# Causal attention's setup: a chunk is projected and split in the norm's own loop, two chunks behind the variances

## What is computed

```python
x = x + _L1_attn_ref(_layernorm(x, axis=-1), Wq, Wk, Wv, Wo)

def _L1_attn_ref(x, Wq, Wk, Wv, Wo):
    q, k, v = (x @ Wq.T), (x @ Wk.T), (x @ Wv.T)     # each to 16 heads of 8
    scores = q @ k.T / sqrt(8), masked so that a query sees no later key
    return (softmax(scores) @ v) @ Wo.T
```

## Time and profile before

| | us |
|---|---|
| median of 3 executions (5180.65 to 5180.82) | 5180.65 |
| the profiled execution | 5180.6 |
| its span in the trace | 5178.8 |
| norm, projection and split of the causal attention (first mean product to first score, L247 to L1397) | 3445.97 to 3535.48 |

### The profile page before, as it was taken

One profiled execution on the slowest core, in us unless ns is written; L12 is line 12 of the kernel. 1 busy time (PEld: TensorE's weight loads), 2 busy tenths in 40 slices (PEclk: granted clock), 3 DMA queues, 4 the chain that ended last, 5 costly groups with the idle time before them and its releaser, 6 DMA issues.

```text
span 5178.8 us, 175419 instructions
## 1 busy us (share of the span) xinstructions
PE 4973.2 (96%) x76384; PEld 3261.6 (63%) x76384; DVE 3878.4 (75%) x5096; ACT 3439.4 (66%) x5293; POOL 2705.8 (52%) x1425
## 2 busy tenths in 40 slices
PE   8899999999999999999999999987999999989999
PEld 5577777777777777777777777762333333267677
DVE  5888888888888888888888888836777777443333
ACT  2588888888888888888888877743655566621111
POOL 1877777777777777777777777721111111110000
PEclk8899999999999999999999999977999999979999
DMA  2011111111111112111111111113111111010000
GB/s 75 25 41 47 33 33 44 43 35 34 36 51 35 30 35 56 31 35 34 44 43 35 30 48 34 35 28 74 20 20 20 20 20 20 1 37 4 4 4 4
DMA packets 98013, 168.30 MB, mean 32 GB/s; under 512 B 25081, under 2 KB 36866, under 8 KB 96898
## 3 DMA queue, kind: packets, MB, share of 16 engines
q1 hardware_dynamic: 94402, 148.06, 10.6%
q10 hardware_dynamic: 2880, 9.44, 1.2%
HBM read 47.44 MB, written 10.49 MB: 11 GB/s over the span
## 4 chain that ended last, share of the span: by engine, by line
PE 88%; ACT 3%; issue 2%; DVE 2%; POOL 1%; SPq 1%; DMA 1%; ACTq 0%; DVEq 0%; POOLq 0%
PE D L1333 7%; PE D L1264 7%; PE D L1189 6%; PE D L1275 6%; PE D L1417 5%; PE D L1439 5%; PE D L1292 5%; PE D L1125 5%; PE D L1243 5%; PE D L1520 5%; PE D L1397 4%; PE D L1301 4%; PE D L1170 4%; PE D L1303 4%; PE D L1178 3%; PE D L1205 2%
## 5 line engine op out<-in xcount | busy, mean ns | idle before, releaser
L475 POOL TENSOR_TENSOR rn<-ss,mhalf 128x33 f32<-128x33 f32 (+2 forms) x198 | 1095.8, 5534 | 329.3 <-DVE ss L861 314.8
L1000 DVE TENSOR_REDUCE mxp<-D 128x2 f32<-128x1024 f32 (+3 forms) x640 | 675.6, 1064 | 242.6 <-PE D L1397 130.9
L479 POOL TENSOR_TENSOR hh<-hh,rr 128x1024 f32<-128x1024 f32 x192 | 365.5, 1904 | 405.9 <-DVE rr L913 405.9
L747 ACT ACTIVATE V<-D 128x1024 f32<-128x1024 f32 (+3 forms) x426 | 381.8, 897 | 248.3 <-PE D L1417 242.7
L968 DVE TENSOR_TENSOR TOK<-D,wA 128x1024 f32<-128x1024 f32 x384 | 466.1, 1214 | 0.0
L859 DVE TENSOR_REDUCE ss<-TOK 128x32 f32<-128x2048 f32 x192 | 437.1, 2276 | 0.0
L1333 PE MATMUL D<-PTb,V 64*64 64x32 f32 x24576 | 406.5, 220 | 8.2 <-issue 7.3
L1333 PEld LDWEIGHTS D<-PTb,V 64*64 64x64 f32 x24576 | 381.6, 135 | 34.8 <-issue 10.8
L908 DVE TENSOR_REDUCE rs<-hh 128x16 f32<-128x1024 f32 x192 | 234.2, 1220 | 205.2 <-ACT hh L647 205.2
L675 ACT ACTIVATE V<-D 128x512 f32<-128x512 f32 x384 | 229.6, 598 | 218.9 <-PE D L1301 153.9
L483 POOL TENSOR_TENSOR XC<-XC,TOK 128x1024 f32<-128x1024 f32 x128 | 302.8, 2366 | 46.5 <-DVE TOK L968 46.5
(11 more groups left out here) (241 smaller groups left out, 11689.1 us busy)
## 6 DMA issues: line engine op xcount, KB each, us to landing
V<-V SPq DMA_DIRECT2D x936, 64.0 KB, 2.0
V<-V SPq DMA_DIRECT2D x192, 192.0 KB, 2.5
RB<-watt_dram SPq DMA_DIRECT2D x12, 512.0 KB, 4.2
X<-watt_dram SPq DMA_DIRECT2D x12, 512.0 KB, 3.8
parts_dram<-hh SPq DMA_DIRECT2D x48, 128.0 KB, 2.4
TOK<-parts_dram ACTq DMA_DIRECT2D x36, 128.0 KB
RA<-parts_dram SPq DMA_DIRECT2D x12, 384.0 KB
X<-parts_dram SPq DMA_DIRECT2D x12, 384.0 KB
```

The costliest lines, as they stand in the source:

```text
L475: pool.tensor_tensor(rn[:, st % 2, lo:hi], ss[:, st % 2, lo:hi], mhalf[:, lo:hi], ALU.pow).then_inc(s["powed"], 1)
L479: pool.tensor_tensor(sh, sh, rr[:, :].unsqueeze(2).to_broadcast([P, HEADS, 64]), ALU.mult).then_inc(s["pnorm"], 1)
L747: act.activation(PTE[i % 3][:, 2 * hp:2 * hp + 2, 0:CH - r * P], pair_of(("S", i + LAG, hp))[:, :].rearrange("p (h n) -> p h n", h=2)[:, : ...
L1000: dve.tensor_reduce(mxp[:, 2 * hp:2 * hp + 2, qt, kc], pair_of(("F", at, hp))[:, :].rearrange("p (h n) -> p h n", h=2)[:, :, 0:keys], AX.X ...
```

## The change

All engines but POOL and SP get the norm's second half (squares, variances, spreads, multiplications) and the projection and split as one loop over steps c. In step c, PE does variance c, spread c-1 and projection c-2; ACT does square c, then high parts and V copy of chunk c-2, then middle parts of chunk c-3; DVE does epsilon c, multiplication c-1, first subtractions of chunk c-2, then second subtractions of chunk c-3. The means and their subtractions stay a loop of their own ahead of it. Since banks 0 to 3 are in use by the norm, q and k go to banks 4 and 5 for every chunk, and v to bank 6 or 7; projection c therefore waits until the first subtractions of chunk c-1 (not c-2) are done. SPL and REST keep two slots. POOL's and SP's programs, and the number and shape of all instructions, are the same.

```diff
--- before.py
+++ after.py
@@ -717,19 +717,28 @@
                                       scr[1, p, hg * GH:(hg + 1) * GH, rep].rearrange("h d n -> d h n"))\
                            .then_inc(s[f"stacks_in{p}"], 16)
 
-            norm_scalar(act, K_ATT, lambda c: chunk(XC, c))
-            for c in range(NC):
-                act.wait_ge(s["c_proj"], c + 1)
-                if c >= 2:
-                    act.wait_ge(s[f"split_out{c % 2}"], 96 * (c // 2))
-                for qk in range(2):
-                    act.activation(SPL[:, c % 2, qk, 0, :], PB[(c % 2) * 3 + qk][:, :], ACT.Copy).then_inc(s["c_hi"], 1)
-                act.activation(VALL[:, c * NBLK:(c + 1) * NBLK, :].rearrange("p b f -> p (b f)"),
-                               PB[(c % 2) * 3 + 2][:, :], ACT.Copy).then_inc(s["c_vcopy"], 1)
-                for qk in range(2):
-                    act.wait_ge(s["c_rest"], 2 * c + qk + 1)
-                    act.activation(SPL[:, c % 2, qk, 1, :], REST[:, c % 2, qk, :], ACT.Copy).then_inc(s["c_mid"], 1)
-                if c == CB:
+            kn = K_ATT * NC
+            for c in range(NC + 3):
+                if c < NC:
+                    act.wait_ge(s["centered"], kn + c + 1)
+                    if c >= 2:
+                        act.wait_ge(s["var_ready"], kn + c - 1)
+                    act.activation(SQ[:, c % 2, :], chunk(XC, c), ACT.Square).then_inc(s["squared"], 1)
+                if 0 <= c - 2 < NC:
+                    u = c - 2
+                    act.wait_ge(s["c_proj"], u + 1)
+                    if u >= 2:
+                        act.wait_ge(s[f"split_out{u % 2}"], 96 * (u // 2))
+                    for qk in range(2):
+                        act.activation(SPL[:, u % 2, qk, 0, :], PB[4 + qk][:, :], ACT.Copy).then_inc(s["c_hi"], 1)
+                    act.activation(VALL[:, u * NBLK:(u + 1) * NBLK, :].rearrange("p b f -> p (b f)"),
+                                   PB[6 + u % 2][:, :], ACT.Copy).then_inc(s["c_vcopy"], 1)
+                if 0 <= c - 3:
+                    u = c - 3
+                    for qk in range(2):
+                        act.wait_ge(s["c_rest"], 2 * u + qk + 1)
+                        act.activation(SPL[:, u % 2, qk, 1, :], REST[:, u % 2, qk, :], ACT.Copy).then_inc(s["c_mid"], 1)
+                if c - 3 == CB:
                     for p in range(2):
                         act.wait_ge(s[f"split_out{p}"], 16 * 6 * CB // 2)
                     act.wait_ge(s["ones_ready"], 3)
@@ -973,19 +982,41 @@
             for st in range(-3, G + 7):
                 att_vector(st)
             dve.wait_ge(s["x2_ready"], NC)
-            norm_vector(dve, K_ATT, lambda c: chunk(XR, c), lambda c: chunk(XC, c))
-            for c in range(NC):
+            kn = K_ATT * NC
+
+            def split_rest(c):
+
                 if c >= 2:
                     dve.wait_ge(s[f"split_out{c % 2}"], 96 * (c // 2))
                 for qk in range(2):
 
                     dve.wait_ge(s["c_hi"], 2 * c + qk + 1)
-                    dve.tensor_tensor(REST[:, c % 2, qk, :], PB[(c % 2) * 3 + qk][:, :], SPL[:, c % 2, qk, 0, :],
+                    dve.tensor_tensor(REST[:, c % 2, qk, :], PB[4 + qk][:, :], SPL[:, c % 2, qk, 0, :],
                                       ALU.subtract).then_inc(s["c_rest"], 1)
+
+            def split_low(c):
+
                 for qk in range(2):
                     dve.wait_ge(s["c_mid"], 2 * c + qk + 1)
                     dve.tensor_tensor(SPL[:, c % 2, qk, 2, :], REST[:, c % 2, qk, :], SPL[:, c % 2, qk, 1, :],
                                       ALU.subtract).then_inc(s["c_low"], 1)
+
+            for c in range(NC):
+                dve.wait_ge(s["mean_ready"], kn + c + 1)
+                dve.tensor_tensor(chunk(XC, c), chunk(XR, c), PB[c % 2][:, :], ALU.subtract).then_inc(s["centered"], 1)
+            for c in range(NC + 3):
+                if c < NC:
+                    dve.wait_ge(s["var_ready"], kn + c + 1)
+                    if c >= 2:
+                        dve.wait_ge(s["rstd_ready"], kn + c - 1)
+                    dve.tensor_scalar(var_s[:, c % 2, :], PB[2 + c % 2][:, 0:NBLK], EPS, None, ALU.add).then_inc(s["var_copied"], 1)
+                if 1 <= c <= NC:
+                    dve.wait_ge(s["spread_ready"], kn + c)
+                    dve.tensor_tensor(chunk(XC, c - 1), chunk(XC, c - 1), PB[(c - 1) % 2][:, :], ALU.mult).then_inc(s["normed"], 1)
+                if 0 <= c - 2 < NC:
+                    split_rest(c - 2)
+                if 0 <= c - 3:
+                    split_low(c - 3)
             dve.wait_ge(s["c_vcopy"], NC)
             dve.memset(PB[4][:, :], 0.0).then_inc(s["o_zero"], 1)
 
@@ -1355,19 +1386,40 @@
                     values(st - 1)
             pe.wait_ge(s["layer_out"], G)
             pe.wait_ge(s["w1att_in"], 16)
-            norm_tensor(pe, K_ATT, lambda c: chunk(XR, c), "x2_ready", lambda c: c + 1)
-            for c in range(NC):
-                pe.wait_ge(s["normed"], K_ATT * NC + (c + 1 if c >= 2 else NC))
+            kn = K_ATT * NC
+
+            def project_c(c):
+
+                pe.wait_ge(s["normed"], kn + c + 1)
+                if c >= 1:
+                    pe.wait_ge(s["c_rest"], 2 * c)
                 if c >= 2:
-                    pe.wait_ge(s["c_rest"], 2 * (c - 1))
                     pe.wait_ge(s["c_vcopy"], c - 1)
-                bk = (c % 2) * 3
-                pe.matmul(PB[bk][:, :], wC[:, 0, :], chunk(XC, c), start=True, stop=True)
-                pe.matmul(PB[bk + 1][:, :], wC[:, 1, :], chunk(XC, c), start=True, stop=True)
+                pe.matmul(PB[4][:, :], wC[:, 0, :], chunk(XC, c), start=True, stop=True)
+                pe.matmul(PB[5][:, :], wC[:, 1, :], chunk(XC, c), start=True, stop=True)
                 for b in range(NBLK):
-                    m = pe.matmul(PB[bk + 2][:, b * P:(b + 1) * P], XC[:, c * CH + b * P:c * CH + (b + 1) * P], wC[:, 2, :],
+                    m = pe.matmul(PB[6 + c % 2][:, b * P:(b + 1) * P], XC[:, c * CH + b * P:c * CH + (b + 1) * P], wC[:, 2, :],
                                   start=True, stop=True)
                 m.then_inc(s["c_proj"], 1)
+
+            for c in range(NC):
+                pe.wait_ge(s["x2_ready"], c + 1)
+                if c >= 2:
+                    pe.wait_ge(s["centered"], kn + c - 1)
+                pe.matmul(PB[c % 2][:, :], mean_w, chunk(XR, c), start=True, stop=True).then_inc(s["mean_ready"], 1)
+            for c in range(NC + 2):
+                if c < NC:
+                    pe.wait_ge(s["squared"], kn + c + 1)
+                    if c >= 2:
+                        pe.wait_ge(s["var_copied"], kn + c - 1)
+                    for j in range(NBLK):
+                        m = pe.matmul(PB[2 + c % 2][:, j:j + 1], SQ[:, c % 2, j * P:(j + 1) * P], mean_w[:, 0:1],
+                                      start=True, stop=True)
+                    m.then_inc(s["var_ready"], 1)
+                if 1 <= c <= NC:
+                    spread(pe, K_ATT, c - 1)
+                if c >= 2:
+                    project_c(c - 2)
             pe.wait_ge(s["tri_ready"], 2)
             pe.wait_ge(s["o_zero"], 1)
             pe.wait_ge(s["c_rest"], 2 * NC)
```

## The result

The changed kernel takes 5197.25 us in the median of 8 executions (5187.81 to 5202.74), the kernel before 5180.65 (8 executions, 5172.38 to 5183.04): a ratio of 1.0033, 95% interval 1.0022 to 1.0043, so 11 to 22 us slower. The profiled execution took 5192.85 us, 12.25 more than the profiled one of before.

What follows compares the result with a forecast made beforehand. Bound: the split's copy, subtract, store ring with two slots. First split 14.76 us earlier, then 11.23 per chunk, an 18.01 store and a 9.09 round put first score 22.9 later: 5203.5 us, range 5187 to 5211.

Steps and rivals of the forecast that it cites:

- Serial order through PE and ScalarE: In the merged norm and split loop, each chunk's steps follow one another through both engines: 11.23 us per chunk.
- The lost slot: In the split's stores, a round of 9.09 us now serves one chunk, not two, and rules from chunk 6 on.
- The tail from there to the first score: From chunk 7's first copy: split 3.42, last subtraction 1.29, memset and semaphores 0.69; 5.40 us predicted.
- The clock: PE in the merged loop was taken at half clock, 0.50, giving 11.23 us per chunk; 8.32 with a full-clock projection.
- rival 2: PE mostly at full clock in the loop: +8.5 us, 5189.1; between, a clock rising inside a projection; chance 0.24.
- Store 4: Store of chunk 4's parts, beside group 0's key and query loads: taken as 18.01 us until chunk 6's first copy.
- the bound of 18.01 + 5: Upper bound in us for chunk 4's store meeting the loads; the lower bound was 5.67, no collision.
- POOL's ones: Memset of the first key stack, 6.92 us, gating the loads: a tie at half clock, some 2 us late at full.
- the time past the first score: Sign for the rest of the kernel: same length as before; a change of over 2 us would show the prediction wrong.
- Rival 4: The loads miss chunk 4's store, which lands in 5.67 us, PE at full clock: -3.8 us, 5176.8; chance 0.04.
- the lower half of rival 2: The part of rival 2 not above 5191, with PE mostly at full clock; 5189.1 us at full.
- slower: Whole kernel slower by more than the 0.2%, 10.4 us, that a measurement can tell from no change; chance 0.82.

Runs made afterwards that it cites:

- experiment 2: Kernel before with only the split staggered: first parts of chunk c, then middle and low parts of chunk c-1; stage 111.1 us, ratio 1.0040.
- experiment 8: Kernel before with only a third slot for the parts; stage 79.3 us, ratio 0.9981.
- experiment 6: Changed kernel with a third slot for the parts, its order kept; stage 101.1 us, ratio 1.0013.
- experiment 1: Changed kernel with chunk c-3's middle and low parts ahead of chunk c-2's first parts; stage 93.0 us, ratio 1.0016.
- experiment 3: Changed kernel with eight thrown-away bfloat16 products ahead of each variance from chunk 3 on; stage 98.2 us, ratio 1.0028.
- experiment 5: experiment 1 with POOL's ones of the first key stack filled ahead of the norm's powers; stage 90.3 us, ratio 0.9996.
- experiment 4: Changed kernel with group 0's query and key loads issued behind the last chunk instead of chunk 4; stage 117.5 us, ratio 1.0059.
- 7: experiment 5 with three slots and group 0's key loads issued ahead of chunk 5's copies; stage 81.7 us, ratio 0.9990.
- 9: Kernel before with four slots and group 0's query loads issued ahead of chunk 4's stores; stage 81.9 us, ratio 0.9976.
- experiment 10: Changed kernel, second parts first, ones early, four slots, key and query loads earlier, six thrown-away products per variance from chunk 3; stage 75.6 us, ratio 0.9969.

## Why the prediction was right, and where it was off

Direction, mechanism and range held: 5203.5 predicted (5187 to 5211), 5197.25 measured; for the stage +22.9 predicted and +15.1 measured. Part of the nearness is luck: two terms were off, one by 12.0 us too much and one by 4.4 too little.

- *Serial order through PE and ScalarE.* Shown: every copy of chunks 1 to 5 was released by the projection, every variance from chunk 4 on waited 3.22 us for its square (3.26 predicted), and turning the order round took 11.5 us away.
- *The lost slot.* Shown by experiment 2 (9.04 to 9.09 us per chunk against 9.09) and by chunk 7's copy, 9.04 after chunk 6's. The tail from there to the first score was 5.31 (5.40 predicted).
- *The clock, the term that was off.* I took 0.50 throughout. The first two projections ran at 1.00, so chunk 0's copy came 17.0 us into the stage (21.5 predicted) and chunk 1's 6.34 later (10.07); and each later projection caught the rise at its end, 10.27 us per chunk on average instead of 11.23. That is 4.5 + 3.7 + 3.8 = 12.0 us too much up to chunk 5. The third part is the case that rival 2 named, a clock that rises inside a projection.

The first two parts are not the change's doing. Up to projection 0 PE has the same instructions in both kernels, and the spread of chunk 0, ahead of any projection, took 1.11 us before and 0.65 after:

```profile
3458.57 1.11 PE L268 MATMUL D<-con,rstd 128*128 128x128 f32 x4 [0.54 <-POOL rstd L304]
```

```profile
3459.93 0.65 PE L268 MATMUL D<-con,rstd 128*128 128x128 f32 x4 [0.54 <-POOL rstd L304]
```

Experiment 8, in the order of before, had 0.65 there as well, and experiment 6, in the changed order, 1.11. So either order met either level at this point, and I had read only the one; in experiment 6 the first copy came at 20.3 us, near the predicted 21.5. Nor does the length of the wait alone decide how a burst begins. In experiment 1 every variance from chunk 3 on waited 2.18 us for its square:

```profile
3465.61 1.05 PE L1416 MATMUL D<-con,SQ 128*128 128x1 f32 x8 [2.18 <-ACT SQ L726]
...
3471.94 1.86 PE L1416 MATMUL D<-con,SQ 128*128 128x1 f32 x8 [2.18 <-ACT SQ L726]
...
3489.55 1.05 PE L1416 MATMUL D<-con,SQ 128*128 128x1 f32 x8 [2.18 <-ACT SQ L726]
```

The first and third of these ran at full clock, the second at half. The Trainium skill, "TensorE: Matmul & The Clock Gate", section "HAM oscillation", describes a loop of short bursts, each behind a wait for a DMA, in which every burst starts throttled. That held from the third burst of the changed kernel on (waits of 3.22 us, 0.57 to 0.58), not for the first two (waits of 2.2 us and less, 1.00). What sets the level in a given execution stays open.

- *Store 4.* 22.4 us instead of 18.01, 4.4 too little, inside the bound of 18.01 + 5. Together: -12.0 + 4.4 is -7.6, the sum's miss of 7.8 but for small change. In experiments 2 and 3 store 4 took 17.9 and 18.0 us beside the same loads; why 22.4 here, no run shows.
- *POOL's ones.* Counted as a tie at half clock and as 2 us late at full. They were 1.1 us late here, and filling them early took 2.7 us off the stage of experiment 1 (experiment 5).
- *A test that was none*: that the time past the first score should stay within 2 us. It changed by 4.5 us, which by that sign would have made the prediction wrong; but it scatters by 12 us among kernels that share that program.
- *A slip in the chances.* Rival 4 and the lower half of rival 2 are 0.04 + 0.12 = 0.16, not 0.14, and "slower" is then 0.80.
- *What I did not see:* that from the issue of the last loads 20 us and more go by. Had the split not been late, they would have set the end; I only had them as a hindrance to the stores.

## What to carry to other kernels

Staggering a producer's stages across chunks (first half of the next ahead of the second half of this one) uses up one buffer slot; where the slots are just enough to cover a store, it turns a round per two chunks into a round per chunk. Before overlapping two stages, ask what the second one really waits for at its end: once the slots sufficed, it was here the start of 2.4 MB of loads, and one more slot in the old order, a few lines, gave about as much (0.9981, interval 0.9972 to 0.9991) as the reordering with the same slots (0.9990, 0.9981 to 0.9999). Before the stage of a single profile is put down to an edit, compare the rows ahead of the edit: here the same instructions differed by 3 us from one execution to another. Work put at the end of an engine's program because it was free there (POOL's ones) has to be looked at again when the loop ahead of it gets longer.

## What the runs showed of the hardware

The loads of group 0 are 1.2 MB of queries and 1.2 MB of keys. From the issue of those that landed last to the first score it took 20.0 us for the queries behind the last stores (experiment 4, the keys issued 13.0 us before), 22.0 and 23.5 for the queries behind chunk 4's stores (6 and 7), 25.5 for the keys in experiment 8, and 27.8 and 28.3 for the keys with the queries issued beside them ahead of chunk 4's stores (9 and 10). A store of 0.8 MB took 5.7 us alone and 18 to 23 beside the loads.

TensorE in a loop with 3.2 us idle and 7 us busy per step was granted 0.57 to 0.58 of its clock in each burst. It had 1.00 when six bfloat16 products were put in the gap, which left 0.9 us of it idle, and the second parts went first, and the loop's step fell from 10.27 to 6.34 us (experiment 10), though in experiment 3 eight such products in a longer step held it only part of the time. Bursts behind one and the same wait of 2.18 us began at either level (experiment 1), and so did the same instructions in different executions (0.65 or 1.11 us for the spread of chunk 0).
